# A two-layer graph kernel on one core: score parts split in the column layout, W·a formed on TensorE, and a new order of the four engines

## What is computed

```python
h  = relu(layernorm(x))
# graph attention, 4 heads, W_heads [4,256,256], a_heads [4,512]
Wh = h @ W[head]
f1, f2 = Wh @ a[head][:256], Wh @ a[head][256:]
e  = leaky_relu(f1[:, None] + f2[None, :]); e = where(adj > 0, e, -1e9)
heads = elu(softmax(e) @ Wh)            # 4 heads side by side: 128 x 1024
out = elu(same attention, one head, W_out [1024,256], a_out [512])
y  = relu(out @ w1 + b1) @ w2 + b2 + out
x2 = x + layernorm(y) * gamma + beta
h3 = relu(layernorm(x2))
result = x2 + deg * (h3 @ Wi.T + b) + adj @ (h3 @ Wj.T)
```

## Time and profile before

| | us |
|---|---|
| median of three runs | 907.75 |
| the profiled execution | 909.05 |
| its span, first to last instruction | 907.2 |
| TensorE (PE) busy in the span | 836.8 (92%) |
| VectorE (DVE) busy | 757.1 (83%) |
| GpSimd (POOL) busy | 703.9 (78%) |
| ScalarE (ACT) busy | 683.0 (75%) |

### The profile page before, as it was taken

How to read it: one execution, slowest core, us unless ns; L and a number is a source line. 1 busy time by engine, 2 the same in 40 slices (tenths; PEclk the granted TensorE clock), 3 DMA queues, 4 the chain that set the end, 5 groups by cost and what they waited for, 6 DMA issues and landing times.

```text
span 907.2 us, 20067 instructions
## 1 busy us (share of the span) xinstructions
PE 836.8 (92%) x6281; PEld 776.6 (86%) x6281; DVE 757.1 (83%) x1998; ACT 683.0 (75%) x1801; POOL 703.9 (78%) x948
## 2 busy tenths in 40 slices
PE   2699999999999999999999999999999999999964
PEld 1589989889998988999898899889889998989952
DVE  4978888898888889888888988888899888897753
ACT  3788878787777878778787877778777877877541
POOL 3587988877788887778888777888877788888852
PEclk9999999999999999999999999999999999999987
DMA  8100010111111011111101111110111111000000
GB/s 246 59 1 24 25 36 2 36 36 36 35 37 35 1 36 36 36 36 36 34 4 36 36 36 36 36 35 3 35 37 36 36 37 35 2 24 25 25 24 23
DMA packets 30136, 31.50 MB, mean 35 GB/s; under 512 B 1856, under 2 KB 28992, under 8 KB 30032
## 3 DMA queue, kind: packets, MB, share of 16 engines
q1 hardware_dynamic: 29776, 29.63, 10.5%
q0 software_dynamic: 256, 0.59, 0.3%
HBM read 21.82 MB, written 8.39 MB: 33 GB/s over the span
## 4 chain that ended last, share of the span: by engine, by line
PE 66%; DVE 17%; issue 9%; POOL 3%; ACT 2%; DMA 1%; SPq 0%; DVEq 0%; POOLq 0%; ACTq 0%
PE ps L1201 59%; DVE g_parts L598 4%; PE ps L1319 3%; DVE wo L711 2%; DVE lend L737 2%; PE ps L1275 2%; PE ps L1393 2%; DVE mj_lo L768 1%; DMA lend<-in_L_gnn_a_heads 1%; ACT mj_hi L1086 1%; DVE c_st L568 1%; DVE g_rest L589 1%; DVE g_parts L621 1%; DVE f_rep L669 1%; PE ps L1341 1%
## 5 line engine op out<-in xcount | busy, mean ns | idle before, releaser
L363 POOL TENSOR_TENSOR h_lo<-h2v,h_hi 128x512 fp32r<-128x512 f32 x128 | 166.6, 1302 | 0.1
L1201 PE MATMUL ps<-gh_hi,wh_hi 128*128 128x256 f32 x512 | 153.7, 300 | 1.6 <-DVE h2v L641 1.1
L1201 PE MATMUL ps<-wo_hi,h_hi 128*128 128x258 f32 x512 | 150.6, 294 | 0.0
L1201 PE MATMUL ps<-wo_lo,h_hi 128*128 128x258 f32 x512 | 145.1, 283 | 0.0
L1201 PE MATMUL ps<-wo_hi,h_lo 128*128 128x258 f32 x512 | 145.0, 283 | 0.0
L1201 PE MATMUL ps<-gh_lo,wh_hi 128*128 128x256 f32 x512 | 142.9, 279 | 0.0
L1201 PE MATMUL ps<-gh_hi,wh_lo 128*128 128x256 f32 x512 | 142.7, 279 | 0.0
L369 POOL TENSOR_SCALAR h2e<-h2e 128x512 f32<-128x512 f32 x128 | 86.2, 681 | 32.0 <-ACT h2e L959 31.8
L1201 PEld LDWEIGHTS ps<-wo_lo,h_hi 128*128 128x128 f32 x512 | 97.4, 190 | 4.3
L1201 PEld LDWEIGHTS ps<-wo_hi,h_hi 128*128 128x128 f32 x512 | 96.8, 189 | 4.6 <-POOL h_lo L363 0.4
L970 ACT ACTIVATE lend<-lend,zm 128x128 f32<-128x128 f32 x256 | 99.1, 393 | 0.0
(11 more groups left out here) (166 smaller groups left out, 2794.3 us busy)
## 6 DMA issues: line engine op xcount, KB each, us to landing
xa<-in_x SPq DMA_DIRECT2D x32, 256.0 KB, 3.1
xr<-in_x SPq DMA_DIRECT2D x32, 256.0 KB, 3.0
out<-res SPq DMA_DIRECT2D x32, 256.0 KB, 2.2
lend<-in_L_gnn_W_heads SPq DMA_DIRECT2D x4, 256.0 KB, 5.7
lend<-in_L_gnn_a_heads SPq DMA_DIRECT2D x4, 256.0 KB, 8.4
wo<-in_L_gnn_W_out SPq DMA_DIRECT2D x1, 1024.0 KB, 11.2
l1w_sb<-in_L_gnn_W SPq DMA_DIRECT2D x1, 512.0 KB, 9.7
lend<-in_L_gnn_w SPq DMA_DIRECT2D x2, 256.0 KB, 3.0
```

The source lines that it names most:

```text
L363: pool.tensor_tensor(h2_lo[:, u, :, :].rearrange("p c n -> p (c n)"), h2v[u % 2][:, :], h2_hi[:, u, :, :].rearrange("p c n -> p (c n)").bi ...
L1201: return pe.matmul(out_, lhs, rhs, start=start, stop=stop)
```

## The change

Four parts, all in one diff:

- The three bf16 parts are made in the column layout, before the transpose. `split_cols` on DVE does five small operations on the 128x16 (second attention: 128x4) values: a float32 copy, the first part, the rest (written back to PSUM), the second part, the third part. Each of the five has one operand in PSUM. The parts go to columns 0, 16 and 32 of a 128x128 bf16 tile whose other columns stay zero; PE transposes it as a bf16 matmul with the identity, and one copy takes it to SBUF (ACT `rows_copy`; DVE `rows2_copy`).
- W·a is formed by PE: a's 16 rows are loaded once (8 KB) and transposed, each head's W is transposed (4 transposes), copied by DVE, and multiplied by a's columns (4 matmuls of 2 columns). The dot products and the four broadcast loads of a go.
- The row constants are loaded by SP instead of POOL's queue.
- The order of every engine and the PSUM banks are new.

```diff
+B_WHT = (0, 1)
+B_WA = 3
...
             def load_heads():
+                sp.dma_start(a_rows[:, :], a_heads.rearrange("h (r o) -> (h r) o", o=P)).then_inc(a_in, 16)
                 for hd in range(H):
                     sp.dma_start(wh[:, :, hd, :], w_heads[hd].rearrange("(c f) o -> f c o", f=P)).then_inc(heads_in[hd], 16)
-                    sp.dma_start(ah_bc[:, hd, :], a_heads[hd].partition_broadcast(P)).then_inc(heads_in[hd], 16)
...
-            def heads_dots(hd):
...
+            def heads_t_copy(hd):
+
+                dve.wait_ge(wh_t_done, hd + 1)
+                if hd >= 2:
+                    dve.wait_ge(wa_done, hd - 1)
+                dve.tensor_copy(wh_t[:, hd % 2, :], ps[:, B_WHT[hd % 2], :]).then_inc(wh_t_copied, 1)
...
+            def split_cols(name, p, cols, whole, parts):
+
+                dve.tensor_copy(whole, cols).then_inc(S[name[0]], 1)
+                dve.tensor_copy(parts[0], cols).then_inc(S[name[1] + "_first"], 1)
+                wait(dve, name[0], p)
+                wait(dve, name[1] + "_first", p)
+                dve.tensor_tensor(cols, cols, parts[0], ALU.subtract).then_inc(S[name[1] + "_rest"], 1)
+                wait(dve, name[1] + "_rest", p)
+                dve.tensor_copy(parts[1], cols).then_inc(S[name[1] + "_second"], 1)
+                wait(dve, name[1] + "_second", p)
+                dve.tensor_tensor(parts[2], cols, parts[1], ALU.subtract).then_inc(S[name[1] + "_third"], 1)
...
+            def rows2_copy(p):
                 wait(dve, "rows2_done", p)
-
                 wait(dve, "scores2_done", p, lag=2)
-                dve.tensor_copy(g_parts[p.e][:, :], ps[:, B_ROWS2, 0:P]).then_inc(S["rows2_first"], 1)
+                dve.tensor_copy(g_parts[p.e][:, :], ps[:, B_ROWS2, 0:P]).then_inc(S["rows2_copied"], 1)
...
+            def heads_products(hd):
+
+                pe.wait_ge(wh_t_copied, hd + 1)
+                pe.wait_ge(a_cols_ready, 1)
+                for c in range(C):
+                    for k in range(C):
+                        last = mm(ps[:, B_WA, 0:COLS].rearrange("p (c j h) -> p c j h", c=C, j=2)[:, c, :, hd],
+                                  wh_t[:, hd % 2, k * F + c * P:k * F + (c + 1) * P], a_cols[:, hd, :, k], k == 0, k == C - 1)
+                last.then_inc(wa_done, 1)
...
-                pe.transpose(ps[:, B_ROWS, 0:P], f_rep[p.e][:, :], ident[:, :]).then_inc(S["rows_done"], 1)
+                mm(ps[:, B_ROWS, 0:P], f_split[p.e][:, :], ident_bf[:, :], True, True).then_inc(S["rows_done"], 1)
```

More of the change, by code:

```diff
@@ L482, in one @@
                     h2_low(p, 2)
-                if p := pairs[0]:
-                    rstd1(p)
+                    h2_low(p, 3)
+                if p := pairs[4]:
+                    out_less(p)
+                if p := pairs[1]:
+                    h_low(p)
+                    soft(p, 0)
+                if p := pairs[5]:
+                    scale2(p)
+                if (p := pairs[4]) and p.is_first():
+                    ffn_low()
+                if p := pairs[4]:
+                    ov_low(p)
             steps(one)
@@ L614, in f_third, with wh2_scores @@
-            def f_third(p):
-                third("rows", p, f_parts, f_rest)
-            def g_first(p):
+                split_cols(("cols_copied", "rows"), p, ps[:, B_COLS, 0:COLS], f_cols[p.e][:, :],
+                           [f_split[p.e][:, k * COLS:(k + 1) * COLS] for k in range(3)])
+            def wh2_scores(p):
+                wait(dve, "wh2_copied", p)
+                wait(dve, "rows2_done", p, lag=1)
+                split_cols(("wh2_scores_copied", "rows2"), p, ps[:, B_WH2[0]:B_WH2[0] + 2, F:WO], g_cols[p.e][:, :, :],
+                           [g_split[p.e][:, k * COLS:k * COLS + 4].rearrange("p (b j) -> p b j", b=2) for k in range(3)])
@@ L789, in one @@
+                if p := pairs[2]:
+                    f_cols_split(p)
+                if p := pairs[5]:
+                    rows2_copy(p)
+                if p := pairs[4]:
+                    elu(p, 1)
+                if p := pairs[3]:
+                    soft_sum(p, 1)
                 if p := pairs[6]:
                     hidden_whole(p)
-                if (p := pairs[0]) and p.is_first():
-                    adj_cast()
-                if p := pairs[2]:
-                    f_cols(p)
@@ new lines, in one @@
+                if p := pairs[6]:
+                    hidden_relu(p)
+                if p := pairs[3]:
+                    at_high(p, 0)
+                if p := pairs[2]:
+                    rows_copy(p)
+                if p := pairs[7]:
+                    norm3(p)
+                if p := pairs[4]:
+                    elu_exp(p, 2)
+                if p := pairs[5]:
+                    score_leaky2(p)
+                if p := pairs[7]:
+                    h3t_high(p)
+                if (p := pairs[3]) and p.is_first():
+                    out_scores_high()
@@ L1468, in one @@
                 if (p := pairs[1]) and p.is_first():
-                    l1w_transposes()
+                    heads_products(2)
                 if p := pairs[4]:
+                    h2_unit(p, 1, 0)
+                if (p := pairs[1]) and p.is_first():
+                    heads_products(3)
+                if p := pairs[4]:
+                    h2_unit(p, 1, 1)
+                if p := pairs[2]:
+                    score_cols(p)
+                if p := pairs[3]:
+                    prob_transposes(p, 0)
@@ new lines, in one @@
+                if p := pairs[6]:
+                    hidden(p, 0)
+                    hidden(p, 1)
+                if p := pairs[5]:
+                    score_rows2(p)
+                if p := pairs[4]:
+                    h2_unit(p, 2, 0)
+                if p := pairs[2]:
+                    score_rows(p)
+                if (p := pairs[0]) and p.is_first():
+                    a_transpose()
+                if p := pairs[5]:
+                    scores2(p)
+                if (p := pairs[0]) and p.is_first():
+                    heads_transposes(0)
```

646 lines of the change are left out of this document (296 added, 350 removed).

## The result

| | before | after |
|---|---|---|
| median of runs, us | 908.16 (907.23 to 909.05, 4 runs) | 878.27 (876.96 to 879.08, 4 runs) |
| profiled execution, us (its span) | 909.05 (907.2) | 876.96 (875.2) |

The ratio is 0.967, 95% interval 0.9653 to 0.9686: 30 us faster, where 36 were forecast. 878.3 us lies inside the range of 863 to 888, and 1 us above the band of 864 to 877 that the forecast itself was given.

What follows compares the result with a forecast made beforehand. PE was taken to set the pace, with nearly all its waiting on g_third. From 909.05 us, 29.6 (waits), 2.6 (returns) and 4 (set-up) came off, giving 872.9, or 872 for the median; range 863 to 888 us.

Steps and rivals of the forecast that it cites:

- The wait: PE's wait on g_third, line 598, lengthened by POOL's lock on DVE: 29 waits of 1.02 us go, 29.6 us.
- The returns: PE's changes back to the large products, 0.08 us each: 9 before, 8 after per step, 2.6 us over 32 pairs.
- The transposes: PE's transposes of the parts as bf16 matmuls: between 0 and 7 us cheaper, taken as 0.
- (a): PE's scores2 behind DVE's rows2_copy: 0.9 us of cover, 0.65 needed, slack 0.2 us.
- (b): PE's score_rows behind DVE's f_cols_split: cover 2.7 us, need 1.3 us, slack 1.4 us.
- (c): PE's h3_transposes behind rows_copy and norm3 on ACT: cover 2.2 us, need 1.8 us, slack 0.4 us.
- The rival of tight waits: One or more short places in the new order fall short by 0.2 to 0.6 us a pair: 878 to 891 us; chance 0.27.
- The residual2 rival: DVE's residual2 held up by POOL's ov_low, 1.27 us more on DVE a pair: 872 to 888 us; chance 0.08.
- fall to the lock: POOL holds the split's small SBUF-writing DVE operations though they read PSUM; 907 or 981 us by size; chance 0.04.
- The set-up: Before the first h2 product: W·a on PE and heads_low moved give 4 us, bounds 0 and 8; start near 39.
- The second 2 us: heads_low, 2.26 us of DVE, moves from the steps of pairs 0 and 1 to before score_cols: another 2 us.
- the drain: Layer norms and splits of the last pair in series, operations unchanged: nothing, +-3 us.

Runs made afterwards that it cites:

- g_third_early: Kernel before with one move: g_third stands directly behind g_second on DVE; 884.76 us, ratio 0.9722.
- rest_in_sbuf: Kernel after, with the rest between the split's parts written to an SBUF tile instead of back into PSUM; 881.87 us, ratio 0.9697.
- split_old_look: Second profile of the kernel before with only the column split, bf16 transposes and rows2_copy, old order and set-up; 893.65 us in one execution.
- changed_again: The kernel after, unedited, run again for comparison on one chip; 878.83 us, ratio 0.9671 to the kernel before.
- dots_setup: Kernel after with W·a again by DVE's dot products and the broadcast loads of a; 879.27 us, ratio 0.9663.
- dots_in_idle: Kernel after with early ACT table load and h transposes, W_out operations moved, W_out dots in DVE's idle time clear of POOL's subtraction; 878.67 us, ratio 0.9661.
- table_and_h_first: Kernel after with a tiny first ACTIVATE loading ACT's table early and pair 0's h transposes before the last products; 878.24 us, ratio 0.9665.
- split_old_order: Kernel before with only the column split, bf16 transposes and rows2_copy, old order and set-up; 893.47 us, ratio 0.9817, median of three agreeing executions.

## Why the prediction was right, and where not

**The wait.** Right, in size and cause. Over the 27 steps from pair 4 to pair 31 the terms give 27 x 1.10 = 29.7 us, and 29.8 are measured. The step was forecast at 25.35 and is 25.38. The returns are 9 a step before and 8 after, as the prediction counted them: one step of each trace has that many large products that follow another kind and cost 0.08 us more than the rest. That g_third was long through POOL, not through its work, is shown by g_third_early (same operation, new place, 0.29 us) and by rest_in_sbuf (small operations stall again once they read SBUF alone). By "SBUF — State Buffer" of the Trainium skill, section "Who interferes with whom", a DVE operation with two SBUF inputs contends with GpSimd, and so does a copy in a two-port mode. The runs agree for both, down to 4 columns.

**The transposes.** Right at the value taken, 0: 0.12 us in bf16 as against 0.11 us.

**The tight places.** (a) was given 0.2 us of slack and has 0.36, (b) 1.4 and has 1.4. For (c), norm3 ends at 440.06 and `h3_transposes` starts at 440.56: 0.5 us, where 0.4 was laid out. The rival of tight waits did not come, but it is near: the old order meets (c) in every pair (split_old_look), and 0.4 us of extra copies meet (a). The residual2 rival did not come either: median 0.692 us. The split did not fall to the lock, because it reads PSUM (rest_in_sbuf shows it).

**The set-up: the step that failed.** It was sized at 4 us, with "What ends last is now ACT" at 14.6 to 15.6 us for `score_cols`. Measured: `score_cols` 1.2 us later than before, the first h2 product 0.7 later (0.3 earlier in changed_again, at 42.99). Two things were wrong. The 17 transposes and the products, put down as lying beside ACT's work, fill PE until 16.7 us: the first 8 transposes take 1.97 us where four of the same form take 0.60 later in the run, so TensorE's pace here is far below that of the rows from which I priced. And ACT's own chain was wrong in two terms that happen to cancel. It left out the table load of 1.28 us, and it counted rowsel (1.91 us), which in fact runs at 18.30, behind `ht_copy`:

```profile
9.65 1.28 ACT L906 ACT_TABLE_LOAD   x1 [9.65 <-DMA lend<-in_L_gnn_W_heads]
10.94 1.91 ACT L906 ACTIVATE wh_hi<-lend 128x2048 fp32r<-128x2048 f32 x1
12.76 1.08 ACT L965 ACTIVATE h<-xa,a_nm,a_rs 128x256 f32<-128x256 f32 x2
```

h is ready at 13.84, where the chain of the prediction gives 12.9 to 13.9: right by luck. PE takes it at 16.71. The second 2 us, for heads_low moved out of the steps, do not show at the first h2 product: behind `score_cols` the dots for W_out hold the first softmax until about 28 us. When they are taken away, the clock takes what they gave, in the execution that was profiled. dots_setup has the same time as the kernel after, which puts W·a on PE at nothing; heads_low stands at its new place in both, so its 2 us were never tested alone. The order has a part in it: split_old_look, with the old order and the old set-up, starts its first h2 product at 41.42, and dots_setup, with the new order and W·a as before, at 43.43. From the first h2 product to pair 4 the kernel after then gains 3.1 us on the kernel before; where, was not followed.

**The sum.** In the profiled executions 32.1 of the forecast 36.2 us came. Outside the 27 steps the forecast holds 6.4 us: 4 for the set-up, two waits of 1.02 in the drain and five returns of 0.08. Of these 2.3 came. About 2 of the missing 4 us lie in the fill. The other 2 lie in the drain, which the prediction put at "nothing" without laying the new order out there: the two waits went, and waits like that of 3.47 us on `ov_low` came. By changed_again more of the loss lies in the drain. The medians differ by 29.9 us: both profiled executions lie some 1 us from their medians, on opposite sides.

That 878.3 us falls inside the range is owed to its upper part, which was there for tight waits that did not come. By its number alone the result would have spoken for that rival (878 to 891 us); the step of 25.38 and the empty waits view speak against it. Of the signs that were laid down, the step, PE's busy time and the split's durations came true; the first h2 product at 37 to 41 us did not.

**Open.** Why the step of g_third_early is 0.35 us above that of the kernel after was not followed beyond its small waits for h2v and the one return more a step (0.08 us). Whether the fill could be shortened with the clock kept up was not tried.

## What to carry to other kernels

Where one DVE operation has a median several times its least, look at what GpSimd runs beside it and at whether all its inputs are in SBUF; moving it, or keeping one operand in PSUM, can each free it. Test the cheap move alone first: here it gave 25 of 30 us. Price the set-up with rows from the set-up, lay a new order out for the fill and the drain too, and expect that time won in a fill with an idle TensorE may be given back by its clock.

## What the runs showed that was not expected

- **The pace of TensorE in the first microseconds.** score_cols, 8 products, takes 1.88 us at 31.24 with the clock at 0.50 in 30 to 35 us, and 0.95 at 46.85 with 1.00. In the kernel before, the windows show 1.00 throughout the first 38 us, yet an aggregation product of 512 columns starts 0.42 us after its predecessor (36.31 to 36.73), while 0.23 is the step later (39.18 to 39.41). The trace says why: its first record of the clock begins at 37.64 us, and the windows view shows 1.00 where there is no record. In the kernel after the first record begins at 26.08 us, in changed_again at 37.91. So ahead of the first record, go by the durations.
- **The clock of the fill differs between like kernels.** The first h2 products are the same in dots_in_idle, changed_again and dots_setup. PE idled 2.69, 1.65 and 1.63 us before them, and they ran at 0.50, 1.00 and 0.50. One profile of each shows it; what decides was not found.
- **A table load waits with its instruction.** ACT's first ACTIVATE waits for W, and its table load of 1.28 us stands behind that wait, at 9.65. Moved to 0.72 us in table_and_h_first, it gave nothing to the total, being off the path.
- **One execution of 2107.86 us.** The kernel split_old_order took it once, beside 892.36, 893.68 and 893.25 us. PE was busy 2070.7 of 2106.1 us, and its products took twice as long throughout (the group of line 1165 on gh_hi and wh_hi 564 ns in the mean against 298 in the kernel after), while the other engines' sums stayed as they were. A pair's step took 64.6 us in place of 25.9. The granted clock of 1.00 that is listed for it says nothing, since its trace holds no record of the clock. The cause is open. It was not seen in the other kernels.
